# A fused attention and mixture-of-experts block: the front rearranged, exponents bounded ahead of the exponential, attention output kept by quarters, shared tiles moved one group forward

## The reference

```python
n = layernorm(x)                                   # over the 512 values
r, k, v = sigmoid(n @ Wr.T), n @ Wk.T, n @ Wv.T
scale = exp(pos * log(clip(sigmoid(decay), 1e-7)))  # per position and channel
state = cumsum(k * v / clip(scale, 1e-10), axis=time) * scale
o = r * state
o = (o - mean(o)) * rsqrt(var(o) + eps)            # over a whole sequence
x = x + (o * gn_weight + gn_bias) @ Wo.T

n = layernorm(x)
top 4 of 64 experts per token by n @ w_router.T, softmax over the 4
each expert takes at most 64 tokens: y = (silu(t @ w_gate) * (t @ w_up)) @ w_down
x = x + weighted sum of the experts' y + (silu(n @ sh_gate) * (n @ sh_up)) @ sh_down
```

## Time and profile before

| | us |
|---|---|
| median of 3 runs (lowest, highest) | 696.11 (696.05, 696.33) |
| the profiled execution | 696.56 |
| its span | 694.7 |
| TensorE matmul busy | 658.8 (95%) |
| VectorE, GpSimd, ScalarE busy | 316.5, 219.8, 162.8 |
| TensorE waits above 1 us in sum, by releaser's line | 9.5 (L981), 2.8 (L1266), 2.2 (L997), 1.5 (L1033), 1.2 (L1080) |

### The profile page before, as it was taken

How to read it: one execution, slowest core, us unless ns; L and a number is a source line. 1 busy time by engine, 2 the same in 40 slices (tenths; PEclk the granted TensorE clock), 3 DMA queues, 4 the chain that set the end, 5 groups by cost and what they waited for, 6 DMA issues and landing times. The chain is left out here.

```text
span 694.7 us, 8795 instructions
## 1 busy us (share of the span) xinstructions
PE 658.8 (95%) x3165; PEld 389.7 (56%) x3165; DVE 316.5 (46%) x750; ACT 162.8 (23%) x268; POOL 219.8 (32%) x210
## 2 busy tenths in 40 slices
PE   4999999999999898999999999999999999999982
PEld 2687878878878753444454454445444444444430
DVE  5887567849958682222233222323323323232321
ACT  5923114633211411211111111112112111111210
POOL 5537446535558222021221220203220122212112
PEclk9999999999999999999999999999999999999997
DMA  8201005722875988999999999999999999999973
GB/s 321 81 7 55 1 31 191 266 74 79 314 265 205 347 325 326 402 405 404 391 399 400 363 399 386 403 369 388 387 405 385 370 385 388 402 396 366 394 225 44
DMA packets 53628, 203.95 MB, mean 294 GB/s; under 512 B 7878, under 2 KB 8262, under 8 KB 53201
## 3 DMA queue, kind: packets, MB, share of 16 engines
q1 hardware_dynamic: 37504, 170.06, 61.3%
q0 software_dynamic: 9072, 21.52, 13.0%
q10 hardware_dynamic: 7008, 11.80, 4.5%
HBM read 179.48 MB, written 24.13 MB: 293 GB/s over the span
## 5 line engine op out<-in xcount | busy, mean ns | idle before, releaser
L657 POOL DMA_INDIRECT out_dram<-ym,midx x32 | 51.3, 1604 | 282.2 <-DVE ym L1266 130.4
L1613 PE MATMUL bank<-w_sb,xT 128*64 128x384 f32 x768 | 129.1, 489 | 0.8 <-ACT xT L884 0.8
L1398 PE MATMUL bank<-x_hi,w_parts 128*128 128x512 f32 x368 | 115.3, 396 | 2.2 <-DVE x_lo L997 2.2
L1613 PEld LDWEIGHTS bank<-w_sb,xT 128*64 128x64 f32 x768 | 53.0, 137 | 71.0 <-issue 67.8
L1398 PEld LDWEIGHTS bank<-x_hi,w_parts 128*128 128x128 f32 x368 | 70.0, 191 | 18.0 <-DVE x_lo L997 3.0
L1398 PE MATMUL bank<-x_lo,w_parts 128*128 128x512 f32 x184 | 71.0, 395 | 0.0
L1201 DVE TENSOR_TENSOR sg<-sg,bank 128x384 f32<-128x384 f32 x32 | 17.8, 555 | 116.6 <-PE bank L1613 62.6
L1531 PE MATMUL bank<-sh_sb,xS 128*128 128x384 f32 x208 | 69.2, 486 | 0.0
L1634 PE MATMUL bank<-w_sb,guT 128*64 128x512 f32 x288 | 65.9, 592 | 2.8 <-DVE ym L1266 2.8
L1531 PEld LDWEIGHTS bank<-sh_sb,xS 128*128 128x128 f32 x208 | 38.7, 191 | 24.1
L911 ACT ACTIVATE y<-bank,wcol 128x512 fp32r<-128x512 f32 x26 | 17.9, 687 | 121.3 <-PE bank L1634 121.3
(11 more groups left out here) (189 smaller groups left out, 939.1 us busy)
## 6 DMA issues: line engine op xcount, KB each, us to landing
w_sb<-in_L_ffn_w_down SPq DMA_DIRECT2D x48, 768.0 KB, 21.1
w_sb<-in_L_ffn_w_gate SPq DMA_DIRECT2D x48, 768.0 KB, 16.6
w_sb<-in_L_ffn_w_up SPq DMA_DIRECT2D x48, 768.0 KB, 19.5
extra<-in_L_ffn_w_gate SPq DMA_DIRECT2D x16, 768.0 KB, 20.1
extra<-in_L_ffn_w_up SPq DMA_DIRECT2D x16, 768.0 KB, 19.9
extra<-in_L_ffn_w_down SPq DMA_DIRECT2D x16, 768.0 KB, 22.7
ring<-in_L_attn_x SPq DMA_DIRECT2D x14, 256.0 KB, 3.7
xS<-xt_dram SPq DMA_DIRECT2D x13, 256.0 KB, 18.2
```

Source lines behind the costliest of these rows:

```text
L657: pool.indirect_dma_start(out=out[:, :], out_offset=bass.IndirectOffsetOnAxis(ap=midx[j % 3][u][:, :], axis=0), in_=ym[u][:, :], in_offset ...
L1398: ins = pe.matmul(ps[u][:, :], w, xp, start=(n == 0), stop=(n == len(parts) - 1))
L1613: ins = pe.matmul(ps[e * C:(e + 1) * C, 0:I], xT[:, c, e * C:(e + 1) * C], gate_up(2 * j + u, e, k)[:, c, :], start=(c == 0), stop=(c == K ...
```

## The change

- **Front.** The decay's logarithm goes to the head of ScalarE's work. VectorE normalises all four tiles first (`xn` of tiles 2 and 3 lies in other free places, and tiles 1, 2 and 3 are turned into other banks), then makes the four `x_lo`. Weights are rounded by channel block: 12 `high` of a quarter of the size, block 0 first; the low parts likewise, each with its own semaphore. Step 0 begins at `x_hi` of four tiles and block 0's high part; its order is now high by high, low weights, then `x_lo`. TensorE runs 14, 9, 8, 2 and 4 unneeded 128x128 transposes of the identity before, between and after the first four turns (`keep_busy`). Tile 6 is normalised before step 0 rather than in it, tile 7 in step 0 rather than step 1.
- **Exponents.** The bound is now `MOST` = ln(1e10) before the exponential; `invert` and its 8 operations are gone.
- **Quarters.** `out_parts` holds high and low of a quarter of the time side by side, so that a place of the expert weights comes free by quarters of the projection; SP loads gate and up of pair 2 after 2, 4 and 6 projections of the second sequence rather than after all 8, and the first half of its down before it waits for the row and the logits.
- **Groups.** `FIRST` is 0: the thirteen shared tiles lie in groups 0 to 12, and groups 13 to 15 have none.

```diff
-FIRST = 1
+FIRST = 0
+MOST = math.log(1e10)
...
+        out_parts = tile("out_parts", [P, 4, 2, KC, 2 * P], F32R, at=out_at)
...
+        def x_bank(n):
+            return (ps_t[0], ps_t[1], ps_k[1], ps_v[1])[n] if n < 4 else ps_t[n % 2 if n < TILES else 1]
+        def xn_place(n):
+            return xw_ring[n - 2] if n in (2, 3) else xn[n % 2]
...
+            sp.wait_ge(y_ready, TILES + 2)
+            fill_matrix(sp, 2, 0, (0,))
+            sp.wait_ge(y_ready, TILES + 4)
+            fill_matrix(sp, 2, 0, (1,))
+            sp.wait_ge(y_ready, TILES + 6)
+            fill_matrix(sp, 2, 1)
             sp.wait_ge(y_ready, 2 * TILES)
-            for k in range(2):
-                load_matrix(2, k)
+            fill_matrix(sp, 2, 2, (0,))
...
+            def low(i, c):
+                pool.wait_ge(hi_ready[i], c + 1)
+                pool.tensor_tensor(w_lo[i][:, c, :, :], outputs(i, c), w_hi[i][:, c, :, :].bitcast(F32),
+                                   ALU.subtract).then_inc(lo_ready[i], 1)
+            pool.wait_ge(xn_ready, 4)
+            low(0, 0)
+            low(0, 1)
+            low(2, 0)
+            low(2, 1)
+            low(0, 2)
+            low(2, 2)
+            powers(1)
+            low(0, 3)
+            powers(1)
+            low(2, 3)
+            powers(1)
...
+            act.wait_ge(setup, 2)
+            act.activation(dec[:, 3, :], dec[:, 2, :], ACT.Ln).then_inc(setup, 1)
             turned_x(0)
+            high(0, 0)
             turned_x(1)
-            high(0)
             turned_x(2)
             turned_x(3)
-            high(1)
-            high(2)
+            high(1, 0)
+            high(0, 1)
+            high(2, 0)
...
-            for n in (4, 5):
+            for n in (4, 5, 6):
                 x_stats(n)
                 x_norm(n)
-            dve.wait_ge(inv_made, KC)
-            invert(0)
...
-                if s + 1 < STEPS:
-                    invert(s + 1)
...
-                        parts = parts[0::3] + parts[1::3] + parts[2::3]
+                        parts = parts[0::3] + parts[2::3] + parts[1::3]
...
+            def keep_busy(count):
+                for _ in range(count):
+                    pe.transpose(ps_r[1][:, 0:P], ident[:, :], ident[:, :])
             pe.wait_ge(ident_steps, 2)
-            for n in range(4):
-                turn_x(n)
+            keep_busy(14)
+            turn_x(0)
+            keep_busy(9)
+            turn_x(1)
+            keep_busy(8)
+            turn_x(2)
+            keep_busy(2)
+            turn_x(3)
+            keep_busy(4)
...
                 if first:
                     down_shared(TAIL - 1)
-                elif shared:
+                if shared:
```

More of the change, by code:

```diff
@@ L20 @@
+import math
 from contextlib import ExitStack
@@ L127, in moe_block, with out_half, out_tile, by_quarter @@
         scale, inv = tile("scale", [P, KC, T], at=scale_at), tile("inv", [P, KC, T], at=inv_at)
-        out_hi, out_lo = (tile(f"out_{n}", [P, KC, T], F32R, at=out_at + i * 4 * K4) for i, n in enumerate(("hi", "lo")))
+        out_parts = tile("out_parts", [P, 4, 2, KC, 2 * P], F32R, at=out_at)
+        def out_half(side, c, h):
+            return out_parts[:, 2 * h:2 * h + 2, side, c, :]
+        def out_tile(side, c, i):
+            return out_parts[:, i // 2, side, c, i % 2 * P:(i % 2 + 1) * P]
+        def by_quarter(ap):
+            return ap.rearrange("p (q t) -> p q t", q=2)
         raw = [tile(f"{n}_raw", [P, KC, D], at=out_at + i * 2 * K4) for i, n in enumerate(("wr", "wv", "wk", "wo"))]
@@ L726, in out_high @@
                 if s == 0:
-                    act.wait_ge(lo_ready, 2)
-                    act.wait_ge(v_lo_ready, 1)
+                    for i in range(3):
+                        act.wait_ge(lo_ready[i], KC)
                 if s == STEPS:
                     act.wait_ge(y_ready, TILES)
-                act.activation(out_hi[:, c, h * HALF:(h + 1) * HALF], r_sb[u][:, :], ACT.Copy).then_inc(outhi_done, 1)
+                act.activation(out_half(0, c, h), by_quarter(r_sb[u][:, :]), ACT.Copy).then_inc(outhi_done, 1)
             def norm_x(n, m):
@@ L988, in x_norm @@
             def x_norm(n):
-                need(dve, xn_turned, n - 1)
-                normalise(xin_place(n)[0], xn[n % 2]).then_inc(xn_ready, 1)
+                if n >= 4:
+                    dve.wait_ge(xn_turned, n - 1)
+                normalise(xin_place(n)[0], xn_place(n)).then_inc(xn_ready, 1)
             def x_low(n):
-                bank_n = n % 2 if n < TILES else 1
                 dve.wait_ge(xhi_ready, n + 1)
@@ L1113, in _ @@
                 x_norm(n - 1)
[L1114 to L1123, removed]
+            x_norm(3)
+            for n in range(4):
+                x_low(n)
             for c in range(KC):
-                ins = dve.tensor_tensor(w_lo[1][:, :, c, :], split(raw[1], c), w_hi[1][:, :, c, :].bitcast(F32), ALU.subtract)
-            ins.then_inc(v_lo_ready, 1)
+                dve.wait_ge(hi_ready[1], c + 1)
+                dve.tensor_tensor(w_lo[1][:, c, :, :], outputs(1, c), w_hi[1][:, c, :, :].bitcast(F32),
+                                  ALU.subtract).then_inc(lo_ready[1], 1)
             dve.wait_ge(setup, 3)
@@ L1336, in turn_x @@
                 pe.wait_ge(xn_ready, n + 1)
-                need(pe, xlo_ready, n - 1 if n < TILES else n)
-                bank_n = n % 2 if n < TILES else 1
+                if n == 5:
+                    pe.wait_ge(rows_copied, 1)
+                if n >= 4:
+                    pe.wait_ge(xlo_ready, n - 1 if n < TILES else n)
                 for c in range(KC):
-                    ins = pe.transpose(ps_t[bank_n][:, c * P:(c + 1) * P], chunk(xn[n % 2][:, :], c), ident[:, :])
+                    ins = pe.transpose(x_bank(n)[:, c * P:(c + 1) * P], chunk(xn_place(n)[:, :], c), ident[:, :])
                 ins.then_inc(xn_turned, 1)
@@ L1347, in output_rows @@
                 pe.wait_ge(raw_in[3], 16)
-                for ps, vector in ((ps_v[1], gnw_sb), (ps_k[1], gnb_sb)):
+                for ps, vector in ((ps_t[1], gnw_sb), (ps_k[1], gnb_sb)):
                     for c in range(KC):
@@ L1383, in step @@
                         continue
-                    if s == 0:
-                        pe.wait_ge(hi_ready, i + 1)
+                    if s < KC:
+                        pe.wait_ge(hi_ready[i], s + 1)
+                    if 0 < s < KC:
+                        pe.wait_ge(lo_ready[i], s + 1)
                     need(pe, free, s - 1)
-                    if s == 1 and i:
-                        pe.wait_ge(rows_copied, i)
+                    if s == 1 and i == 2:
+                        pe.wait_ge(rows_copied, 2)
                     parts = []
```

68 lines of the change are left out of this document (31 added, 37 removed).

## The result

The changed kernel is slightly slower. Its median over 20 runs is 696.97 us (695.29 to 701.16), against 696.10 us (695.47 to 697.94) for 20 runs of the kernel before: a ratio of 1.0016, 95% interval 1.0009 to 1.0024. The forecast of 690.9 was wrong in size and in sign. The profiled execution has a span of 695.7 us, against 694.7. Further down, one execution each of e2, e7, e8 and e9 took far longer than its fellows (710.00, 986.36, 770.69 and 2398.81 us) and is left out of their medians and ratios.

A forecast was written before the change was run, and what follows sets the result against it. Bound: TensorE's pitch of 0.227 us a matmul between front and groups, and the chain of adds into DRAM at the end. Front 4.5 + adds 0.7 = 5.2 us, span 694.7 to 689.5, forecast 690.9 us, range 688.8 to 694.7.

The forecast's parts named there:

- The head of the front: Front, clock up early: step 0 begins at 12.4 us and ends at 20.8, 4.6 earlier.
- the late case: Front, clock rising only near the third tile's turn: step 0 at 14.0 us, its end at 22.3, 3.1 earlier.
- So `x_lo` of tile 4 stays near its 36.81 to 37.5: Front: VectorE has one more norm (about 2.2 us) before it; TensorE newly waits 0.7 us before tile 6's turn.
- the wait of 0.77 at 60.16: TensorE's wait for tile 7's `x_lo` before step 4 goes; lasting gain of the front taken as 4.5 us.
- VectorE and GpSimd hold the front: Rival in the front: GpSimd's low parts delay norms, tile 4's `x_lo` 2 us later, front gains 2.5: 692.9 us; chance 0.18.
- worth nothing: VectorE's 8 removed clip operations, up to 1.50 us each, gain nothing, as VectorE waits for TensorE from step 4 on.
- Storing by quarters: Projection output: same counts written and read, so zero; smaller blocks might cost ScalarE and GpSimd tens of ns.
- Gain on TensorE: zero: Early loads of pair 2 add no wait and gain TensorE nothing; the weight stream begins about 1.9 us ahead.
- TensorE's sum: zero: Groups: a shared tile's 7.2 us moves from group 13 to group 0, leaving TensorE's total unchanged.
- The adds: Chain of adds into DRAM at the end: last one at 685.7 us against 686.64, 0.9 earlier; 0.7 taken.
- the third rival: Adds set the end later: eleven intervals without slack, at 1 us more under load 698.9 us; chance 0.06.
- One replaces the other: Group 14's new wait for the vector copy, 2.5 to 3 us, replaces the wait of 2.78 at 672.79.

The follow-up runs named there:

- e2: The kernel before with only the shared tiles moved to groups 0 to 12 (`FIRST` = 0): 697.00 us, ratio to the kernel before 1.0015.
- e7: The changed kernel with 36 unneeded transposes ahead of group 14's first `down_pair`: 696.76 us, ratio to the kernel before 1.0009.
- e8: The changed kernel with the four `wo_lo` made before steps 3 and 4, not 1 and 2: 693.72 us, ratio to the kernel before 0.9967.
- e9: The changed kernel with `wo_lo` two steps later and `FIRST` = 1: 691.46 us, ratio to the kernel before 0.9931.
- e4: The changed kernel with tiles 6 and 7 turned inside steps 2 and 3: 697.40 us, ratio to the kernel before 1.0022.
- e12: e9 with tile 6 normalised in step 0 and tile 7 in step 1, as before: 694.06 us, ratio to the kernel before 0.9968.
- e10: The changed kernel with `FIRST` = 1 and pair 2's weights loaded as before: 695.79 us, ratio to the kernel before 0.9997.
- e1: The changed kernel with its shared tiles back in groups 1 to 13 (`FIRST` = 1): 694.83 us, ratio to the kernel before 0.9991.
- e3: The changed kernel without the five `keep_busy` calls (unneeded transposes): 695.58 us, ratio to the kernel before 1.0009.
- e5: The kernel before with only the unneeded transposes added around its first turns: 697.25 us, ratio to the kernel before 1.0013.

## Why the prediction was wrong, point by point

- **The head of the front: right.** Step 0 at 12.40 for 12.4, the rows at 20.69 for 20.8, with the clock up early. In other executions (e4, e7, e9, e12) step 0 started at 13.1 to 13.8, inside the 14.0 of the late case.
- **"So `x_lo` of tile 4 stays near its 36.81 to 37.5 ... a new wait of 0.7": the step that failed, with the next one.** It ended at 38.4, and the wait was 1.52. I had one more norm at 2.2; it took 3.2 (29.31 after 26.15), because each `xn` of tiles 4 to 6 took 1.43 and not 0.55: those of tiles 4 and 5 beside the low parts that the change put between GpSimd's powers (29.17), that of tile 6 beside the product of v with the inverse scale. In the kernel before the low parts were done before these norms.
- **"In its place the wait of 0.77 at 60.16 ... goes ... because ... VectorE's step 2 come sooner": half right.** That wait went, but a wait of 2.30 for tile 5's `x_lo` came, which was in no term. The 4.6 on TensorE only meant something if each later operand of VectorE came 4.6 earlier, and I checked that for tile 4 alone. Then 1.6 us went to the low clock behind the wait. In numbers: 4.5 at step 1, less 3.82 of waits against 0.20 and 0.77 before, less 1.6, is 0.1, and 0.2 was measured at 99 us for a forecast of 4.5. The rival "VectorE and GpSimd hold the front" had the mechanism, and still left 2.5.
- **The clip "worth nothing": nearly so, but not for the reason given.** The cover named, VectorE waiting from step 4 on, isn't there in steps 0 to 3. The one between `x_lo` of tiles 4 and 5 took 1.42, but `wo_lo` then met GpSimd in its place and grew by 1.07, which leaves about 0.3. No run tested it alone. "Storing by quarters ... zero" was right as far as the trace tells: ScalarE's copy to `out_parts` takes 0.63 where that to `out_hi` took 0.62.
- **Loads of pair 2, "Gain on TensorE: zero": right for TensorE's front, wrong for the end.** By e10 they shorten the stream's end and so the last adds, by about 1 us (not clear of the noise) with `FIRST` = 1; with `FIRST` = 0 the DMA engines idle their lead away.
- **"TensorE's sum: zero" of the groups: nearly.** Group 13 starts 7.57 later for 7.2, group 14 0.38 later; TensorE's own work cost no more than that.
- **The adds.** From 590.45 the second add of group 12 was due at 644.1 and came at 644.72. From there the forecast took plain intervals of 9.56, 9.10 and 9.10; they were 9.67, 9.51 and 9.79. I had the idle of 0 to 2 us in the early groups (it is 10 x 0.25 = 2.5 from 280 to 290) but carried it nowhere: it is 1.4 of the 2.3 MB that come back among the last adds. The other 0.9 is moved less from 290 to 350 with the engines as full as in e1; why, no run shows. Without the front's gain the last add was due at 685.7; it came at 687.65, 0.6 of that lost by 644.72 and 1.3 behind it. (The eleven intervals of the third rival against eight are counted unlike: counted like the eleven there were nine.)
- **"One replaces the other": the place right, the size wrong.** The wait in group 14 was 3.70 for a forecast of 2.5 to 3, with 1.74 of low clock behind it. Against 2.78 before, that is 2.7 lost.
- **Sum.** In the profiled executions the front's 4.5 came to 0.2, and the 0.7 of the adds to a loss of 1.2: together 1.0 slower for a forecast of 5.2 faster. By the medians: the front rearranged with bound and quarters, but neither early loads nor `FIRST`, -0.2 (e10); early loads -1.0 (e1 against e10); `FIRST` = 0 +2.1 (the changed kernel against e1). That these make the measured +0.9 proves nothing, since each is the difference to the next kernel; of the three, only the last is clear of the noise.

## What to carry to other kernels

Time won at the head of a pipeline counts only as far as every later operand from the other engines moves with it: walk down all waits, not the next one, with the contended duration of each operation, and move work that nobody wants yet (here `wo_lo`) out of the full stretch first. A wait that takes another's place may cost more than its length, if the clock falls behind it (here 1.6 and 1.7 us). At a tail of chained adds, count the bytes that are still to load: what the stream doesn't move early it moves between the last adds.

## What the runs showed of the hardware

- Dense transposes raise TensorE's clock: the first turn of four took 0.75 with 14 transposes ahead of it and 1.10 in e3 without, and step 0's first eight products 2.11 against 3.78. It is not the same each time: in e4, e5, e7, e9 and e12 the first turn took 1.13 with the same 14 ahead of it, and the clock was up only by the third turn (0.64 or 0.65).
- After waits of 2.30 (49.75) and 3.70 (654.37) in the changed kernel, 2.84 in e4, 2.27 in e1, 2.67 in e5 and 3.41 in e3 the granted clock fell, at 1.6 and 1.7 us in the changed kernel; after 2.78 in the kernel before, 2.98 in e2, 2.28 in e7 and 3.37 in e4 it did not. The length of the wait alone doesn't decide it. The changed kernel's runs spread over 5.9 us and those of the kernel before over 2.5, and the spread goes with the clock: the mean granted clock was 0.985 and 0.986 in its two longest executions (700.50 and 701.16) and 0.992 or 0.993 in its five shortest. Where it fell in those isn't recorded.
- The adds into DRAM take 4.75 us from issue to landing once the weights have ended and 8.72 among them (644.72).
